# Transposing DMAs in place of TensorE for the normalised rows, with GpSimd taking half of the y rounding

## Chip, cores, metric

One core of a Trainium2 chip. The metric is the device time of one execution in microseconds (us), the median of several runs.

## What is computed

x is 4 x 2048 x 512 (batch, sequence, hidden), all in f32. Two branches start from the same normalised x and meet at the end:

```
xn  = layernorm(x)
q, k, v = xn @ Wq.T, xn @ Wk.T, xn @ Wv.T            # 512 -> 128 each
scan over the sequence:  r_t = q_t @ M.T ;  M = 0.99 * M + v_t.T @ k_t / b
s   = (r @ Wo.T) * sigmoid(gate)
h   = layernorm(xn) * gamma + beta
y   = silu(h @ dequant(fc1_q, fc1_scales) + fc1_bias)     # 512 -> 2048, scale groups of 128
z   = y @ dequant(fc2_q, fc2_scales) + fc2_bias           # 2048 -> 512, scale groups of 128
g   = silu(xn + 0.5 * z)
out = x + s * g
```

## The kernel before

The sequence is cut into 16 **chunks** of 128 steps: 4 batches x 128 steps are 512 rows, four tiles of 128. Precision is kept by splitting f32 operands into two f16 parts, a high one (the value rounded) and a low one (what rounding left), so most products are two or three f16 matmuls. Scales of groups are applied between partial sums: a bank is multiplied in place by a ratio before the next group is added to it.

Five instruction streams are written out by hand in **slots**, 64 to a chunk (`STEPS`), `G` counting all slots and `e` the slot in its chunk. No scheduler changes the order: what stands in a stream waits there, and all behind it waits too. The engines meet at semaphores only.

- **Every slot, TensorE**: one piece of fc1 (`ffn1`, L490, two matmuls) and one of fc2 (`ffn2`, L508, two matmuls). Block J of fc1 (128 of the 2048 features) takes four pieces two slots apart; even blocks have their last piece at slots 6, 14, 22, ..., odd blocks at 3, 11, 19, ... Two banks `blk` alternate between blocks.
- **ScalarE** multiplies each fc1 bank by its ratio (`rescale`, L636), which the next piece of that block waits for two slots later, and after the fourth piece makes y (`silu`, L643).
- **VectorE** multiplies each fc2 bank by its ratio (`block2_out`, L776; four banks, so TensorE wants each back after four slots), and splits y: `y_high` (L762) in the slot after silu, `y_low` (L767) in the slot after that. Both are needed by fc2 of the block, and `silu` of the block after next waits for `y_low`.
- **Side jobs, TensorE**: q at slot 3 (L439); for the four tiles, starting at slots 1, 13, 25, 37: kv (L450), kt (L455), scores (L460), read (L467 to L469) and wo (L475), 0, 4, 7, 10 and 13 slots after the start. They share two side banks.
- **Normalising the next chunk**: VectorE takes `stats` (L730) of x in slots 0 to 3 and `moments` (L733) in slots 5 and 6. GpSimd makes the row constants (`rows`, L1035 to L1045, then `row_scales`, L1053) and writes g = (x - mean) * scale into `g_rows` (`normalise`, L1060). TensorE **turns** g in slots 51, 54, 56, 59 (`turn`, L426): four transposes each into a side bank. From that bank ScalarE copies the high part (`g_high`, L583) and makes h (`h_whole`, L592), VectorE makes g's low part (`g_low`, L746), GpSimd splits h (`h_high` L1072, `h_low` L1076). fc1 of the next chunk needs h from its slot 0 on, kv and q need g from its slot 1 on.
- **Finishing the chunk before**, on GpSimd mostly: `prepare` (L1102, L1105) makes xn plus half the bias, `add_z` (L1110) adds z; ScalarE takes the last silu (`gate_silu`, L662, slots 16, 17, 21, 29); `output` (L1116, L1119) multiplies by s and adds x (slots 18, 22, 26, 30). GpSimd's order within a chunk is prepare 0 and 1, rows, add 0 and 1, prepare 2, add 2, prepare 3, output 0, add 3, outputs 1 to 3, four normalises, four splits of h.
- **SyncE** issues all loads and stores: of the next x (`load_x`, once g is made), of the x for the end (`load_again`), and the output.

In chunk 0 GpSimd, VectorE and ScalarE also unpack the fc2 weights; chunk 15 has no next chunk to normalise. The first chunk's g is turned before slot 0, in another place of the program (L547).

## Time and profile before

| | us |
|---|---|
| median of 3 runs | 1266.86 (1266.81 to 1268.67) |
| the profiled execution, its own time | 1264.73 |
| its span | 1262.8 |
| TensorE busy | 1190.5 (94%) |
| VectorE busy | 1143.2 (91%) |
| ScalarE busy | 914.7 (72%) |
| GpSimd busy | 784.3 (62%) |
| clock granted to TensorE | 0.993 of full |

The profiler's "busy" of TensorE counts the overlapping ends of pipelined matmuls, so the distance from one matmul's start to the next one's start says what it costs the stream. In the profile PE is TensorE, DVE VectorE, ACT ScalarE, POOL GpSimd, SP SyncE. `side`, `blk`, `blk2` are banks; the profile leaves buffer numbers out.

### The profile page before, as it was taken

How to read it: one execution, taken by the hardware profiler on the slowest of the kernel's cores; microseconds unless marked ns; L12 is line 12 of the kernel's file. 1: busy time of each engine (PE TensorE's matmuls, PEld its weight loads, DVE VectorE, ACT ScalarE, POOL GpSimd, SP SyncE). 2: the span in 40 equal slices, each digit the busy share in tenths (PEclk: the TensorE clock that was granted, in tenths of full speed). 3: DMA queues.
4: the chain of work that ended last, by engine and by line, in shares of the span. 5: the costliest groups of instructions: out<-in, count | busy, mean ns of one | idle time of the engine just before them, and what ended most of it. 6: DMA issues, size and time to landing. Idle time of an engine off the chain costs nothing.

```text
span 1262.8 us, 18949 instructions
## 1 busy us (share of the span) xinstructions
PE 1190.5 (94%) x6028; PEld 616.7 (49%) x6028; DVE 1143.2 (91%) x1969; ACT 914.7 (72%) x1590; POOL 784.3 (62%) x760
## 2 busy tenths in 40 slices
PE   2799999999999999999999999999999999999994
PEld 1344554555555555555555545555455545555551
DVE  8889989899998999999899998989999899999897
ACT  6788776777777767676777777677777776768672
...
DMA packets 41620, 65.68 MB, mean 52 GB/s; under 512 B 11696, under 2 KB 11952, under 8 KB 41008
## 3 DMA queue, kind: packets, MB, share of 16 engines
...
q10 hardware_dynamic: 288, 0.08, 0.0%
...
## 4 chain that ended last, share of the span: by engine, by line
PE 73%; DVE 12%; ACT 8%; issue 5%; POOL 1%; DMA 1%; SPq 0%; ACTq 0%; DVEq 0%
PE blk L490 27%; PE blk L508 25%; PE side L450 6%; DVE blk L776 5%; PE side L475 4%; PE side L439 3%; ACT blk L636 3%; PE side L467 2%; DVE y_split L767 2%; DVE tops L814 2%; ACT z_rows L662 1%; PE side L426 1%; DVE y_split L762 1%; PE side L468 1%; PE side L469 1%
## 5 line engine op out<-in xcount | busy, mean ns | idle before, releaser
L776 DVE TENSOR_TENSOR blk<-blk,ratio_rows 128x512 f32<-128x512 f32 x960 | 646.0, 692 | 79.4 <-PE blk L508 75.8
L636 ACT ACTIVATE blk<-blk,ratio 128x512 f32<-128x512 f32 x768 | 508.2, 666 | 228.9 <-PE blk L490 222.8
L490 PE MATMUL blk<-h_split,q_sb 128*128 128x512 f16 x2048 | 611.1, 380 | 12.1 <-ACT y_full L643 4.2
L508 PE MATMUL blk<-w_sb,y_split 128*128 128x512 f16 x2048 | 608.7, 379 | 2.5 <-POOL w_sb L1081 1.3
L508 PEld LDWEIGHTS blk<-w_sb,y_split 128*128 128x128 f16 x2048 | 199.4, 98 | 247.4 <-DVE blk L776 7.3
L490 PEld LDWEIGHTS blk<-h_split,q_sb 128*128 128x128 f16 x2048 | 194.4, 98 | 224.1 <-ACT blk L636 32.5
L643 ACT ACTIVATE y_full<-blk,par,last 128x512 f32<-128x512 f32 x256 | 201.6, 787 | 82.6 <-PE blk L490 81.9
L767 DVE SCALAR_TENSOR_TENSOR y_split<-y_full,up,y_split 128x512 f16<-128x512 f32 x256 | 220.6, 862 | 0.1
L1072 POOL CAST h_split<-h_full 128x512 f16<-128x512 f32 x64 | 52.6, 822 | 239.8 <-ACT h_full L592 239.8
L762 DVE TENSOR_SCALAR y_split<-y_full,up 128x512 f16<-128x512 f32 x256 | 170.1, 665 | 0.0
L1060 POOL TENSOR_SCALAR g_rows<-xt,mv,gs 128x512 f32<-128x512 f32 x60 | 133.1, 2227 | 0.0
L1116 POOL TENSOR_TENSOR z_rows<-z_rows,s_rows 128x512 f32<-128x512 f32 x62 | 92.2, 1488 | 58.7 <-ACT z_rows L662 58.7
L1110 POOL TENSOR_TENSOR z_rows<-z_rows,xz 128x512 f32<-128x512 f32 x60 | 90.3, 1513 | 12.0 <-DVE z_rows L781 10.8
L1119 POOL TENSOR_TENSOR z_rows<-z_rows,x_again 128x512 f32<-128x512 f32 x62 | 84.8, 1368 | 4.9
L1105 POOL TENSOR_TENSOR xz<-xz,b_half 128x512 f32<-128x512 f32 x60 | 83.2, 1386 | 5.0
L1076 POOL TENSOR_TENSOR h_split<-h_full,h_split 128x512 f16<-128x512 f32 x64 | 74.6, 1165 | 5.2
L450 PE MATMUL side<-wqkv_hi,g_hi 128*128 128x256 f16 x256 | 70.3, 275 | 1.5 <-DVE wqkv_lo L942 1.5
L450 PE MATMUL side<-wqkv_lo,g_hi 128*128 128x256 f16 x256 | 70.4, 275 | 0.0
L450 PE MATMUL side<-wqkv_hi,g_lo 128*128 128x256 f16 x256 | 70.4, 275 | 0.0
L781 DVE SCALAR_TENSOR_TENSOR z_rows<-blk,unit,ratio_rows 128x512 f32<-128x512 f32 x64 | 47.6, 744 | 22.3 <-PE blk L508 22.3
L475 PE MATMUL side<-wo_sb,s_mask 128*128 128x512 f32 x128 | 65.5, 593 | 0.5 <-DVE mem_t L756 0.5
L1102 POOL TENSOR_SCALAR xz<-x_again,row_z 128x512 f32<-128x512 f32 x60 | 56.9, 949 | 0.0
...
## 6 DMA issues: line engine op xcount, KB each, us to landing
xt<-in_x SPq DMA_DIRECT2D x64, 256.0 KB, 4.6
x_again<-in_x SPq DMA_DIRECT2D x256, 64.0 KB, 1.9
out<-z_rows SPq DMA_DIRECT2D x256, 64.0 KB, 1.7
...
```

The lines of the kernel that those rows point to most:

```text
L450: mm = pe.matmul(bank[:, 0:2 * M], a[:, k, rows], w[:, k, M:], start=(k == 0 and n == 0), stop=(k == KC - 1 and n == 2))
L475: pe.matmul(bank[:], r_t[:], wo_sb[:], start=True, stop=True).then_inc(wo_done, 1)
L490: mm = pe.matmul(blk[J % 2][:], q1_sb[:, g, j // 4, w, j % 4 * P:(j % 4 + 1) * P], a[:, c % 2, g, :], start=(g == 0 and n == 0), stop=(g = ...
L508: mm = pe.matmul(blk2[:, i, :], y[:, J % Y_RING, rows], w2_sb[:, j, part, :], start=(j == 0 and n == 0), stop=(j == FB - 1 and n == len(te ...
L636: act.activation(blk[J % 2][:], blk[J % 2][:], ACT.Copy, scale=ratio1[:, at:at + 1]).then_inc(blk_scaled, 1)
L643: act.activation(y_full[:, J % 2, :], blk[J % 2][:], ACT.Silu, bias=b1_c[:, j:j + 1], scale=last1[:, j:j + 1]).then_inc(silu_done, 1)
L762: dve.tensor_scalar(y_hi[:, J % Y_RING, :], y_full[:, J % 2, :], up_y, None, ALU.mult).then_inc(y_hi_done, 1)
L767: dve.scalar_tensor_tensor(y_lo[:, J % Y_RING, :], y_full[:, J % 2, :], up_y, y_hi[:, J % Y_RING, :], ALU.mult, ALU.subtract).then_inc(y_l ...
L776: dve.tensor_tensor(blk2[:, i, :], blk2[:, i, :], ratio2_rows[:, j, :], ALU.mult).then_inc(blk2_scaled, 1)
L1060: pool.tensor_scalar(g_rows[:, i, :], xt[:, i, :], mv[:, c % 2, i, 0:1], gs[:, c % 2, i:i + 1], ALU.subtract, ALU.mult).then_inc(g_done, 1)
L1110: pool.tensor_tensor(z_rows[:, i, :], z_rows[:, i, :], xz[:, i % 2, :], ALU.add).then_inc(z_sum, 1)
L1116: pool.tensor_tensor(z_rows[:, i, :], z_rows[:, i, :], s_rows[:, n % S_RING, :], ALU.mult).then_inc(z_mul, 1)
```

## The change

g no longer goes through TensorE, except for the first chunk. GpSimd's `normalise` writes g in place of x, in the form x * scale + shift, in slots 31, 33, 35, 37; the shift costs two more steps of `rows`, which moves from slot 7 to 9. ScalarE rounds the rows to the high part (`g_high`, slots 33 to 39), GpSimd subtracts (`g_low`, slots 34 to 40), and SyncE issues eight DMAs that transpose 128 x 512 of f16 each into `g_hi` and `g_lo` (`turn_g`). h is then made of g's two parts: `h_part` on ScalarE (slots 48, 50, 52, 54), `h_sum` on VectorE one slot later, the split on GpSimd one slot after that. `y_high` of odd blocks goes to GpSimd (`odd_y_high`), at slots 4, 12, 20, ..., and their `y_low` on VectorE from slot 5, 13, ... to slot 7, 15, ... The statistics stand at slots 0, 2, 4, 6, and the moments at 7 and 8.

```diff
-TURN_AT = (51, 54, 56, 59)
...
+G_HIGH_AT, G_LOW_AT = (33, 35, 37, 39), (34, 36, 38, 40)
+H_PART_AT, H_SUM_AT, H_SPLIT_AT = (48, 50, 52, 54), (49, 51, 53, 55), (50, 52, 54, 56)
...
-STATS_AT, MOMENTS_AT = (0, 1, 2, 3), (5, 6)
+STATS_AT, MOMENTS_AT = (0, 2, 4, 6), (7, 8)
...
-MASK_LAG, MEM_LAG, GLOW_LAG, YHIGH_LAG, YLOW_LAG = 1, 1, 3, 1, 2
-
-HSPLIT_LAG = 3
-NORMALISE_AT = (36, 38, 40, 42)
-PREPARE_AT, ROWS_AT, FIRST_ROWS_AT = (0, 3, 15, 18), 7, 28
+MASK_LAG, MEM_LAG, YHIGH_LAG, YLOW_LAG, ODD_YLOW_LAG = 1, 1, 1, 2, 4
+
+NORMALISE_AT = (31, 33, 35, 37)
+PREPARE_AT, ROWS_AT, FIRST_ROWS_AT = (0, 3, 15, 18), 9, 28
...
+        g_rows = xt
+        g_split = sb("g_split", [P, 2, NT, H], F16)
...
+            def turn_g(c):
+
+                sp.wait_ge(h_done, 4 * c)
+                sp.wait_ge(kv_done, 4 * c)
+                sp.wait_ge(q_done, c)
+                for i in range(NT):
+                    sp.wait_ge(g_lo_rows, NT * (c - 1) + i + 1)
+                    for n, to in enumerate((g_hi, g_lo)):
+                        sp.dma_start_transpose(to[:, :, i * P:(i + 1) * P], g_split[:, n, i, :]).then_inc(g_turned, 16)
...
                 if 0 < c < NCH - 1:
-                    g_wait(sp, c)
+                    sp.wait_ge(g_lo_rows, NT * c)
                     load_x(c + 1)
...
+                if c < NCH - 1:
+                    turn_g(c + 1)
...
+            def g_high(c, i):
+                act.wait_ge(g_done, NT * c + i + 1)
+
+                wait(act, g_turned, 2 * NT * 16 * (c - 1))
+                act.activation(g_split[:, 0, i, :], g_rows[:, i, :], ACT.Copy).then_inc(g_hi_rows, 1)
+
+            def h_part(c, k):
+                act.wait_ge(g_turned, 2 * NT * 16 * c)
+                act.wait_ge(h_done, 4 * c + k - 1)
+                act.activation(h_full[:, k % 2, :], g_hi[:, k, :], ACT.Identity,
+                               bias=beta_s[:, k:k + 1], scale=gamma_s[:, k:k + 1]).then_inc(h_part_done, 1)
...
+            def h_sum(c, k):
+                dve.wait_ge(h_part_done, 4 * (c - 1) + k + 1)
+                dve.scalar_tensor_tensor(h_full[:, k % 2, :], g_lo[:, k, :], gamma_s[:, k:k + 1], h_full[:, k % 2, :],
+                                         ALU.mult, ALU.add).then_inc(h_full_done, 1)
...
             def y_low(J):
-                dve.wait_ge(y_hi_done, J + 1)
+                if J % 2:
+                    dve.wait_ge(y_hi_odd_done, J // 2 + 1)
+                else:
+                    dve.wait_ge(y_hi_done, J // 2 + 1)
...
-                pool.tensor_tensor(nmr[:, c % 3, :], t[3], row_const[:, MINUS_ONE, :], ALU.mult
+                step(pool.tensor_tensor(nmr[:, c % 3, :], t[3], row_const[:, MINUS_ONE, :], ALU.mult))
+                step(pool.tensor_tensor(t[3], mean, gs[:, parity, :], ALU.mult))
+                pool.tensor_tensor(g_shift[:, parity, :], t[3], row_const[:, MINUS_ONE, :], ALU.mult
                                    ).then_inc(rows_done, 1)
...
-                    pool.wait_ge(turn_done, 4 * c)
-                pool.tensor_scalar(g_rows[:, i, :], xt[:, i, :], mv[:, c % 2, i, 0:1],
-                                   gs[:, c % 2, i:i + 1], ALU.subtract, ALU.mult).then_inc(g_done, 1)
+                pool.tensor_scalar(g_rows[:, i, :], xt[:, i, :], gs[:, c % 2, i:i + 1],
+                                   g_shift[:, c % 2, i:i + 1], ALU.mult, ALU.add).then_inc(g_done, 1)
+
+            def g_low(c, i):
+                pool.wait_ge(g_hi_rows, NT * (c - 1) + i + 1)
+                pool.tensor_tensor(g_split[:, 1, i, :], g_rows[:, i, :], g_split[:, 0, i, :], ALU.subtract
+                                   ).then_inc(g_lo_rows, 1)
...
+            def odd_y_high(J):
+                if J == 1:
+                    pool.wait_ge(y_scale, 1)
+                wait(pool, blk2_done, NT * (J - Y_RING + 1))
+                pool.wait_ge(silu_done, J + 1)
+                pool.tensor_scalar(y_hi[:, J % Y_RING, :], y_full[:, J % 2, :], up_y, 1.0, ALU.mult, ALU.mult
+                                   ).then_inc(y_hi_odd_done, 1)
```

Three places of the new order. On GpSimd, from the sum for the last tile of the chunk before (`add_z` of tile 3, slot 20) to the second normalise, before:

```order
L1110 TENSOR_TENSOR z_rows<-z_rows,xz 128x512 [waits z_out,xz_done]
L1116 TENSOR_TENSOR z_rows<-z_rows,s_rows 128x512 [waits s_out,z_silu]
L1119 TENSOR_TENSOR z_rows<-z_rows,x_again 128x512 [waits z_mul]
L1116 TENSOR_TENSOR z_rows<-z_rows,s_rows 128x512 [waits s_out,z_silu]
L1119 TENSOR_TENSOR z_rows<-z_rows,x_again 128x512 [waits z_mul]
L1116 TENSOR_TENSOR z_rows<-z_rows,s_rows 128x512 [waits s_out,z_silu]
L1119 TENSOR_TENSOR z_rows<-z_rows,x_again 128x512 [waits z_mul]
L1060 TENSOR_SCALAR g_rows<-xt,mv,gs 128x512 [waits turn_done,rows_done]
L1060 TENSOR_SCALAR g_rows<-xt,mv,gs 128x512 x3
```

and now (`y_split<-y_full` is the high half of an odd block):

```order
L1118 TENSOR_SCALAR y_split<-y_full,up 128x512 [waits silu_done,blk2_done]
L1149 TENSOR_TENSOR z_rows<-z_rows,xz 128x512 [waits z_out,xz_done]
L1155 TENSOR_TENSOR z_rows<-z_rows,s_rows 128x512 [waits s_out,z_silu]
L1158 TENSOR_TENSOR z_rows<-z_rows,x_again 128x512 [waits z_mul]
L1155 TENSOR_TENSOR z_rows<-z_rows,s_rows 128x512 [waits s_out,z_silu]
L1158 TENSOR_TENSOR z_rows<-z_rows,x_again 128x512 [waits z_mul]
L1118 TENSOR_SCALAR y_split<-y_full,up 128x512 [waits silu_done,blk2_done]
L1155 TENSOR_TENSOR z_rows<-z_rows,s_rows 128x512 [waits s_out,z_silu]
L1158 TENSOR_TENSOR z_rows<-z_rows,x_again 128x512 [waits z_mul]
L1084 TENSOR_SCALAR xt<-xt,gs,g_shift 128x512 [waits rows_done]
L1084 TENSOR_SCALAR xt<-xt,gs,g_shift 128x512
L1089 TENSOR_TENSOR g_split<-xt,g_split 128x512 [waits g_hi_rows]
```

Two high halves of y stand within this piece, a third ahead of it (slot 12), and g's low part follows the second normalise.

On ScalarE, slots 31 to 36 of the same chunk, now:

```order
L648 ACTIVATE blk<-blk,ratio 128x512 [waits blk_done] x3
L599 ACTIVATE g_split<-xt 128x512 [waits g_turned,g_done]
L648 ACTIVATE blk<-blk,ratio 128x512 [waits blk_done]
L655 ACTIVATE y_full<-blk,par,last 128x512 [waits y_lo_done,blk_done]
L599 ACTIVATE g_split<-xt 128x512 [waits g_turned,g_done]
L648 ACTIVATE blk<-blk,ratio 128x512 [waits blk_done]
```

The rescale of slot 34 stands behind a wait for the first normalise (`g_done`); before, no instruction of ScalarE stood behind `normalise` until slot 52.

On SyncE, now:

```order
L352 DMA x_again<-in_x 32x512 x4
L373 DMA_TRANSPOSE g_hi<-g_split 128x4x128 [waits q_done,g_lo_rows,kv_done,h_done]
L373 DMA_TRANSPOSE g_lo<-g_split 128x4x128
L373 DMA_TRANSPOSE g_hi<-g_split 128x4x128 [waits g_lo_rows]
L373 DMA_TRANSPOSE g_lo<-g_split 128x4x128
L373 DMA_TRANSPOSE g_hi<-g_split 128x4x128 [waits g_lo_rows]
L373 DMA_TRANSPOSE g_lo<-g_split 128x4x128
L373 DMA_TRANSPOSE g_hi<-g_split 128x4x128 [waits g_lo_rows]
L373 DMA_TRANSPOSE g_lo<-g_split 128x4x128
L345 DMA xt<-in_x 32x4x512 [waits g_lo_rows]
```

The load of the next x, which stood behind the normalises alone, now stands behind the eight transposing DMAs, and these behind kv of the last tile (slot 37).

## Rows read from the trace of the kernel before

**Rows 1.** Page, span and busy time of each engine.

```profile
span 1262.8 us, 18949 instructions
PE 1190.5 (94%) x6028; PEld 616.7 (49%) x6028; DVE 1143.2 (91%) x1969; ACT 914.7 (72%) x1590; POOL 784.3 (62%) x760
```

**Rows 2.** Stretches of one chunk each: length, busy time by engine, clock, DMA.

```profile
485.34:560.22 74.88, 73.58 (x377) 38.40 (x377) 68.39 (x117) 55.05 (x98) 48.90 (x47) 1.00 0.16 43
560.22:635.10 74.88, 73.58 (x376) 38.37 (x377) 68.39 (x117) 55.06 (x98) 48.90 (x47) 1.00 0.17 43
```

**Rows 3.** Chain of waits, 605 to 640 us: start, us, what.

```profile
606.06 0.43 PE blk L490 x2
606.50 0.43 PE blk L508 x2
...
626.71 0.44 PE side L426 x4
...
632.20 0.39 DVE y_split L762
632.59 0.61 DVE blk L776
633.19 0.65 DVE y_split L767
...
634.45 0.60 DVE g_lo L746
...
635.10 0.66 PE side L426 x4
```

**Rows 4.** TensorE by time, fc1 of slots 0, 8, 36, fc2 of slot 6.

```profile
564.49 0.60 PE L490 MATMUL blk<-h_split,q_sb 128*128 128x512 f16 x2 [0.16 <-ACT y_full L643]
...
574.12 0.59 PE L508 MATMUL blk<-w_sb,y_split 128*128 128x512 f16 x2
...
575.42 0.59 PE L490 MATMUL blk<-h_split,q_sb 128*128 128x512 f16 x2
...
608.71 0.59 PE L490 MATMUL blk<-h_split,q_sb 128*128 128x512 f16 x2
```

**Rows 5.** GpSimd by time, 576 to 615 us: start, us, line, [idle before it].

```profile
576.23 0.20 POOL L1035 TENSOR_TENSOR v<-mv,row_const 128x4 f32<-128x4 f32 x1 [5.34 <-DVE mv L733]
...
581.82 0.20 POOL L1045 TENSOR_TENSOR row_z<-v,row_const 128x4 f32<-128x4 f32 x1
...
585.53 0.77 POOL L1102 TENSOR_SCALAR xz<-x_again,row_z 128x512 f32<-128x512 f32 x1
586.39 1.27 POOL L1105 TENSOR_TENSOR xz<-xz,b_half 128x512 f32<-128x512 f32 x1
...
591.58 1.27 POOL L1116 TENSOR_TENSOR z_rows<-z_rows,s_rows 128x512 f32<-128x512 f32 x1
592.92 1.33 POOL L1119 TENSOR_TENSOR z_rows<-z_rows,x_again 128x512 f32<-128x512 f32 x1
...
603.27 1.66 POOL L1116 TENSOR_TENSOR z_rows<-z_rows,s_rows 128x512 f32<-128x512 f32 x1 [1.68 <-ACT z_rows L662]
...
606.51 8.86 POOL L1060 TENSOR_SCALAR g_rows<-xt,mv,gs 128x512 f32<-128x512 f32 x4
```

**Rows 6.** VectorE by time, the last moments of the chunk.

```profile
575.92 0.24 DVE L733 BATCH_NORM_AGGREGATE mv<-stat 128x2 f32<-128x6 f32 x2
```

**Rows 7.** Groups by line and shape: busy us, mean ns of one, idle before.

```profile
L583 ACT ACTIVATE g_hi<-side 128x512 f16<-128x512 f32 x60 | 36.1, 602 | 0.0
L1145 POOL TENSOR_SCALAR b_half<-b_half 128x512 f32<-128x512 f32 x1 | 1.5, 1512 | 0.0
```

**Rows 8.** y's low half on VectorE: shortest, median and longest in ns.

```profile
L767 DVE SCALAR_TENSOR_TENSOR y_split<-y_full,up,y_split x256: 735/747/1648, 47.4 to 1241.6; 128x512 f16<-128x512 f32 x128
```

**Rows 9.** DMA issues: KB each, us to landing; then SyncE by time.

```profile
xt<-in_x SPq DMA_DIRECT2D x64, 256.0 KB, 4.6
x_again<-in_x SPq DMA_DIRECT2D x256, 64.0 KB, 1.9
...
596.07 1.83 SPq L349 DMA_DIRECT2D x_again<-in_x  x4
```

More of the change, by code:

```diff
@@ L20 @@
 TOP = 2.0 ** 14
-ROW_STEPS = 10
+ROW_STEPS = 12
 TINY = 1e-30
@@ L69 @@
         SIDE[TILE_AT[_i] + JOB_AT[_n]] = (_job, _i)
-    SIDE[TURN_AT[_i]] = ("turn", _i)
 def build(nc, x, wqkv, wo, gate, m0, q1, q2, b2, params, out):
@@ L91, in side_job @@
             return None
-        job, i = SIDE[e]
-        c += 1 if job == "turn" else 0
-        return (job, c, i) if c < NCH and not (job == "turn" and c == 0) else None
+        return (SIDE[e][0], c, SIDE[e][1]) if c < NCH else None
     def job_behind(G, lag, kind):
@@ L106, in finishing, with next_chunk @@
         return (c - 1, at.index(e)) if c > 0 and e in at else None
+    def next_chunk(G, at):
+        c, e = divmod(G, STEPS)
+        return (c + 1, at.index(e)) if c < NCH - 1 and e in at else None
     def fc1_step(G):
@@ L417, in bank_free @@
                     pe.wait_ge(s_out, n)
-                else:
-                    pe.wait_ge(g_lo_done, n)
-            def turn(c, k, bank):
-                if k == 0:
-                    g_wait(pe, c)
-                for i in range(NT):
-                    mm = pe.transpose(bank[:, i * P:(i + 1) * P], g_rows[:, i, k * P:(k + 1) * P], ident[:])
-                mm.then_inc(turn_done, 1)
             def run_side(G):
@@ L432, in run_side @@
                 bank_free(G)
-                if job == "turn":
-                    turn(c, i, bank)
-                elif job == "q":
+                if job == "q":
                     for k in range(KC):
@@ L442, in run_side @@
                 elif job == "kv":
-                    if i == 0:
-                        pe.wait_ge(g_lo_done, 4 * c + 4)
+                    if i == 0 and c == 0:
+                        pe.wait_ge(g_lo_done, 4)
+                    elif i == 0:
+                        pe.wait_ge(g_turned, 2 * NT * 16 * c)
                     if c == 0 and i == 0:
@@ L682, in _ @@
             for k in range(KC):
-                h_whole(0, k, first_turn_bank[k])
-                g_high(0, k, first_turn_bank[k])
+                first_h(k, first_turn_bank[k])
+                first_g_high(k, first_turn_bank[k])
             act.wait_ge(wqkv_scale, 1)
@@ L717, in _ @@
                     s_copy(*at, side[JOB_BANK[G - S_LAG]])
-                if at := job_behind(G, GHIGH_LAG, "turn"):
-                    g_high(*at, side[JOB_BANK[G - GHIGH_LAG]])
-                if at := job_behind(G, HFULL_LAG, "turn"):
-                    h_whole(*at, side[JOB_BANK[G - HFULL_LAG]])
+                if at := next_chunk(G, G_HIGH_AT):
+                    g_high(*at)
+                if at := next_chunk(G, H_PART_AT):
+                    h_part(*at)
                 if at := finishing(G, GATE_AT, LAST_GATE_AT):
@@ L924, in _ @@
             top_of_q1(3).then_inc(tops_made, 1)
-            g_low(0, 0, first_turn_bank[0])
+            first_g_low(0, first_turn_bank[0])
             pick(OF_Q1)
-            g_low(0, 1, first_turn_bank[1])
+            first_g_low(1, first_turn_bank[1])
             largest(OF_Q1, top_q1[:])
@@ L975, in _ @@
                     mask_scores(*at, side[JOB_BANK[G - MASK_LAG]])
-                if at := job_behind(G, GLOW_LAG, "turn"):
-                    g_low(*at, side[JOB_BANK[G - GLOW_LAG]])
+                if at := next_chunk(G, H_SUM_AT):
+                    h_sum(*at)
                 if at := job_behind(G, MEM_LAG, "read"):
                     remember(*at, side[JOB_BANK[G - MEM_LAG]])
-                if (at := fc1_step(G - YHIGH_LAG) if G >= YHIGH_LAG else None) and at[1] == KC - 1:
+                if (at := fc1_step(G - YHIGH_LAG) if G >= YHIGH_LAG else None) and at[1] == KC - 1 and at[0] % 2 == 0:
                     y_high(at[0])
-                if (at := fc1_step(G - YLOW_LAG) if G >= YLOW_LAG else None) and at[1] == KC - 1:
+                if (at := fc1_step(G - YLOW_LAG) if G >= YLOW_LAG else None) and at[1] == KC - 1 and at[0] % 2 == 0:
+                    y_low(at[0])
+                if (at := fc1_step(G - ODD_YLOW_LAG) if G >= ODD_YLOW_LAG else None) and at[1] == KC - 1 and at[0] % 2:
                     y_low(at[0])
@@ L1148, in _ @@
                 c, e = divmod(G, STEPS)
+                if (at := fc1_step(G - YHIGH_LAG) if G >= YHIGH_LAG else None) and at[1] == KC - 1 and at[0] % 2:
+                    odd_y_high(at[0])
                 if G - Q2_LOW_LAG in Q2_AT:
@@ L1161, in _ @@
                     row_scales(c + 1)
-                if c < NCH - 1 and e in NORMALISE_AT:
-                    normalise(c + 1, NORMALISE_AT.index(e))
-                if at := job_behind(G, HSPLIT_LAG, "turn"):
+                if at := next_chunk(G, NORMALISE_AT):
+                    normalise(*at)
+                if at := next_chunk(G, G_LOW_AT):
+                    g_low(*at)
+                if at := next_chunk(G, H_SPLIT_AT):
                     h_high(*at)
```

47 lines of the change are left out of this document (21 added, 26 removed).

## The prediction

> **What bounds the kernel now.** I read the page's busy times first: TensorE is busy for 94% of the span, VectorE for 91%, GpSimd for 62% [rows 1]. Stretches of one chunk each then show a steady state: two chunks in a row last 74.88 us, at full clock, with the same counts [rows 2]. So the sum can be made for one chunk. The chain of waits shows what such a chunk is: in most slots TensorE follows TensorE, 0.43 us for the two matmuls of fc1 and 0.43 us for those of fc2 [rows 3]. Where the turns stand the chain leaves TensorE: a turn costs the stream 0.44 us when its bank is free, and before the fourth it waits for `g_low`, 0.66 instead of 0.44 us in the chain, with about 0.34 us lost at that place [rows 3]. Slot 0 loses about 0.33 us more behind a silu (TensorE idle, released by ScalarE) [rows 4]. The last view is GpSimd by time. It waits 5.34 us for the moments, starts the row constants at 576.23 us, and from there to the first normalise at 606.51 us is idle once, for 1.68 us before the last product [rows 5]. That stretch is the one to keep in mind: nobody waits for its end now, since g is turned only at 626.71 us [rows 3]. A measurement of this kernel can tell changes of about 0.2% (2.5 us) from none.
>
> **What TensorE gains.** Four turns of 0.44 us leave each chunk: 1.76 us. With them goes the 0.34 us before the fourth. The 0.33 us at slot 0 comes from ScalarE being crowded by eight extra instructions between slots 52 and 61; it has the same eight afterwards, four (`g_high`) in slots 33 to 39 and four (`h_part`) in slots 48 to 54, so I take it to go and put 0.3 us back for new small waits. Gain if nothing else gets in the way: 1.76 + 0.34 + 0.33 - 0.30 = 2.1 us a chunk.
>
> **What VectorE gains, priced at nothing.** It loses eight `y_high` of 0.39 us and four `g_low` of 0.60 us a chunk and gets four `h_sum`; by its operands the nearest row to that is `y_low`, 0.65 us [rows 3]. That is about 3 us less in 68.4 us of work [rows 2]. It is hidden by TensorE except around the turns, counted above. If the gain did not come, the cover is the four slots for which a bank of fc2 may be away.
>
> **What moves onto the path: GpSimd between slots 8 and 33.** `g_high` on ScalarE stands in slot 33 and waits for the first normalise. The rescale of slot 34 stands behind it, and TensorE needs that rescale for fc1 in slot 36. So a late normalise stops TensorE. I count from the start of slot 8 (575.42 us now [rows 4]).
>
> - The moments end two slots later than now. VectorE starts from the fc2 product of slot 6 (574.12 + 0.63 us [rows 4]) and has three scalings of 0.61, one statistics of about the same, one `y_high` 0.39, two `y_low` 0.65 and two pairs of moments of 0.24 [rows 3, 6]: done near 579.4 us, 3.9 us after the start of slot 8. Now it is 576.2 us.
> - GpSimd's stretch now takes 606.51 - 576.23 = 30.3 us; without the idle 1.68 it is 28.6 us of work [rows 5]. Added are two row steps of 0.28 us each (a 0.20 us step and the gap to the next), three high halves of y (slots 12, 20, 28), and the first normalise itself, which must now be complete. The new normalise has the form of L1102, multiply and add with two columns of scalars: 0.77 us [rows 5], a third of the old one's 8.86 / 4. For the high half no row has two multiplies. The nearest from below is L1102, 0.77 us; the old normalise (subtract, multiply) took 2.2 us, and the one single multiply, L1145, 1.51 us [rows 5, 7]. I take 0.77, the row with the same count of operations and a multiply first, and keep 2.2 for a rival. Sum: 28.6 + 0.56 + 2.31 + 0.77 = 32.2 us.
> - Part of the 28.6 is mutual hindrance. `y_low` takes 735 ns at the shortest and up to 1648 ns [rows 8], and GpSimd's own instructions are stretched next to VectorE's. Unhindered, the stretch has 6.1 us of row constants, two preparations of 0.77 + 1.27 and their gaps (2.1), four outputs of 1.27 + 1.33 (2.6) and four adds of 1.3 [rows 5], together 25.9 instead of 28.6: then 29.5 instead of 32.2. Fewer `y_high` on VectorE take a part of the 2.7 us away, I say a quarter: 31.5 us.
> - Behind it: `g_high` 0.60 us [rows 7], one rescale of about 0.6, a semaphore's delay: 1.3 us.
>
> Slot 36 then starts 3.9 + 31.5 + 1.3 = 36.7 us after slot 8. Now it is 608.71 - 575.42 = 33.3 us [rows 4]. That is 3.4 us lost a chunk; smaller waits on the way (the gate's silu in slots 16 and 17 behind `add_z`, `y_low` of slot 23 behind the high half of slot 20) fall inside it, because GpSimd is late, not held up by them.
>
> The Trainium skill says in "SBUF — State Buffer", on contention, that VectorE and GpSimd share one port pair as an exclusive lock, held for a whole instruction, when VectorE runs a two-port mode or reads two SBUF tensors. By that rule `h_sum` (two SBUF inputs) brings new collisions with the splits of h in slots 49 to 56, and an odd `y_high` on VectorE was one itself; the spread of `y_low` agrees with it. It changes the 0.3 us put back above, perhaps to 1.
>
> **The transposing DMAs.** Eight of 128 KB each chunk. They may start when kv of the last tile is done, about 3.2 us after slot 36 starts, and must all have landed when ScalarE comes to `h_part` in slot 48, about 14.7 us after it: a window of 11.5 us. The last pair is released by the fourth `g_low` some 7 us before its end. No transposing DMA is in the trace. From below: an issue costs SyncE 1.83 / 4 = 0.46 us and 64 KB land in 1.9 us, 256 KB in 4.6 us [rows 9]; one after the other issued, overlapping in flight, the eight fit. From above: eight that each take 4.6 us alone need 36.8 us. I take them to fit, since the DMA engines are only 16 to 17% busy [rows 2], and price them at nothing; the cover is the 11.5 us. The next load of x, queued behind them, lands in 4.6 us and is wanted a good 15 slots later.
>
> **Sum.** A steady chunk: 3.4 - 2.1 = +1.3 us, 74.9 to 76.2. There are 14 such chunks: +18. Chunk 0 has nothing to finish and keeps 2.1 us of gain; chunk 15 has no normalise but the odd high halves among its GpSimd work, about +1.5. Together +17: the profiled execution's 1264.7 becomes 1282, and the median, which lies 2.1 us above it, 1284.
>
> **Rivals.**
> - **GpSimd is in time (faster).** Place: slot 33. The first normalise decides; ScalarE gets there about 29.4 us after slot 8 and has 1 us to spare, so at 30.4 us nothing is lost and at 35.4 (my 3.9 + 31.5) the 3.4 us are. Unhindered it is 33.4, slot 36 is 1.4 us later instead of 3.4, and the sum is -0.7 a chunk: 14 of them and the -0.6 of the two ends give 1256. If the stretch is shorter still, because the moments come as early as now or the hindrance was mine to overrate, up to 2.1 us a chunk come in, 15 x 2.1 = 32: 1235. For it: TensorE is the busiest engine and its work shrinks for certain. Against: the stretch is already without gaps and only gets longer.
> - **The high half of y is slow on GpSimd.** At 1.5 to 2.2 us instead of 0.77 the three in the stretch add 2.2 to 4.3 us a chunk: 1284 + 14 x 2.2 = 1315 to 1344. For it: two of the three nearest rows. Against: the fast one shares its opening multiply by a column of scalars.
> - **The transposes are late.** They decide once the eight take over 11.5 us. At 1.9 us each, one after the other, they take 15.2: 3.7 us more a chunk, 15 times: 1340. At 4.6 us each it is 25 us a chunk, beyond 1600. For it: no row shows one overlapping another. Against: the idle DMA engines.
>
> The Trainium skill's page "VectorE: DVE Perf Modes", in "The three transpose paths", gives 1309 ns for a 128 x 128 square of 2-byte values by DMA against 390 ns on TensorE, and prefers TensorE; should that be a cost in sequence, the 32 squares of a chunk would need an estimated 42 us, near the worst of this rival. The page "DMA: Bandwidth & Descriptors" gives 261 GB/s for one kernel's DMA transposes, by which a chunk's megabyte would take an estimated 4 us, which fits.
>
> **How the numbers follow.** Forecast 0.45, its own range 1260 to 1304 (a stretch near 29.8, and 32.2 with 1 us of new waits). In time: 0.27, 1235 to 1260. Slow high half: 0.12. Late transposes: 0.16, half of that beyond 1345. The range 1238 to 1342 leaves out less than 2 in 10. Faster by over 0.2%: 0.27 and a sixth of the forecast, 0.34. Within 0.2%: 0.08, from the forecast. Slower: 0.58.
>
> **What would show it.** Right: ScalarE idle before `g_split<-xt` of slot 33, released by GpSimd, some 3 us, and TensorE's wait for the rescale behind it; GpSimd without a gap from the row constants to the normalise; a steady chunk of 76 us. Wrong: a chunk under 74 us with that idle time absent; `y_split<-y_full` on GpSimd over 1.2 us; ScalarE idle before `h_full<-g_hi`, released by a DMA, which would be the transposes.

## The result, and the profile after

The change takes **1353.4 us** (median of four runs, 1352.4 to 1354.2) against 1266.9 for the kernel before: 1.0681 times as long, interval 1.0668 to 1.0694. Forecast were 1284 and a range of 1238 to 1342. The sign is right; the loss is 87 us where 17 were forecast.

The page of the changed kernel, its span, busy times and the chain by engine (before: [rows 1]):

```profile
span 1351.8 us, 18739 instructions
PE 1192.6 (88%) x5788; PEld 590.6 (44%) x5788; DVE 1124.2 (83%) x1842; ACT 927.9 (69%) x1590; POOL 861.4 (64%) x980
...
PE 42%; POOL 23%; DVE 18%; issue 12%; ACT 4%; DMA 1%; POOLq 0%; SPq 0%; ACTq 0%; DVEq 0%
```

TensorE is no longer at 94% but at 88%, and no other engine has taken its place as the busiest. Less than half of the chain is TensorE's. That is the picture of engines that wait for one another. Two chunks, each from the start of its slot 0 to the start of the next slot 0 (length, busy time by engine, clock, DMA; before: [rows 2]):

```profile
527.09:606.79 79.70, 72.41 (x362) 36.23 (x361) 67.12 (x109) 55.82 (x98) 53.47 (x61) 1.00 0.23 54
606.79:687.95 81.16, 74.10 (x362) 36.71 (x361) 66.90 (x109) 56.00 (x98) 53.66 (x61) 0.98 0.22 53
```

There are two kinds of chunk now. Of chunks 1 to 14, five take 79.7 us with the clock at 1.00, and nine 81.0 to 81.2 us with the clock at 0.98; before, all took 74.9 at 1.00. Together the fourteen take 1128.8 us instead of 1048.4, 80 of the 89 us that the span is longer; chunk 0 takes 90.5 instead of 83.3. So most of the loss lies in the steady chunk: 4.8 us in each, and 1.5 us more where the clock fell. The view of waits (engine, line, for whom; us in all, times, longest):

```profile
POOL v L1058 <- DVE mv L745: 125.9, 15, 8.8
POOL h_split L1101 <- DVE h_full L761: 108.4, 29, 7.0
...
DVE y_split L786 <- POOL y_split L1118: 44.4, 14, 3.2
PEld side L480 <- DVE mem_t L772: 43.3, 15, 3.0
...
PE side L480 <- DVE mem_t L772: 35.9, 15, 2.5
...
ACT h_full L604 <- POOL h_split L1105: 19.9, 15, 1.5
...
ACT g_split L599 <- POOL xt L1084: 15.1, 15, 1.3
```

Once in each chunk VectorE waits 3.2 us in `y_low` (L786) for GpSimd's high half (L1118), and once TensorE waits 2.5 to 3 us in wo (L480) for VectorE's memory update (L772). The wait that the prediction named, ScalarE before `g_split<-xt` (L599), is there too, at 1.0 us rather than 3. The timelines of one chunk (the second above) show how the first two hang together. GpSimd:

```profile
621.62 0.20 POOL L1058 TENSOR_TENSOR v<-mv,row_const 128x4 f32<-128x4 f32 x1 [8.42 <-DVE mv L745]
...
637.74 1.44 POOL L1155 TENSOR_TENSOR z_rows<-z_rows,s_rows 128x512 f32<-128x512 f32 x1
639.26 1.27 POOL L1158 TENSOR_TENSOR z_rows<-z_rows,x_again 128x512 f32<-128x512 f32 x1
640.51 0.69 POOL L1118 TENSOR_SCALAR y_split<-y_full,up 128x512 f16<-128x512 f32 x1
...
650.12 1.27 POOL L1155 TENSOR_TENSOR z_rows<-z_rows,s_rows 128x512 f32<-128x512 f32 x1 [1.10 <-ACT z_rows L674]
...
652.73 2.70 POOL L1084 TENSOR_SCALAR xt<-xt,gs,g_shift 128x512 f32<-128x512 f32 x2
```

VectorE in the same place:

```profile
637.50 0.56 DVE L778 TENSOR_SCALAR y_split<-y_full,up 128x512 f16<-128x512 f32 x1
641.24 1.74 DVE L786 SCALAR_TENSOR_TENSOR y_split<-y_full,up,y_split 128x512 f16<-128x512 f32 x1 [3.17 <-POOL y_split L1118]
642.90 0.69 DVE L795 TENSOR_TENSOR blk<-blk,ratio_rows 128x512 f32<-128x512 f32 x1
643.50 0.27 DVE L772 SCALAR_TENSOR_TENSOR mem_t<-mem_t,side 128x128 f32<-128x128 f32 x1
```

And TensorE:

```profile
643.83 1.60 PE L480 MATMUL side<-wo_sb,s_mask 128*128 128x512 f32 x2 [2.54 <-DVE mem_t L772]
645.22 1.06 PE L495 MATMUL blk<-h_split,q_sb 128*128 128x512 f16 x2
```

The high half of slot 20 stands on GpSimd behind two steps of an output tile and starts at 640.51. VectorE has come to the low half (slot 23) at 638.07 and stands for 3.17 us. Behind it in VectorE's queue, after one scaling of a bank, is the 0.27 us memory update. It reads the bank into which wo of slot 26 will write, so TensorE waits for it. A product of GpSimd that is late by three microseconds stops TensorE through two queues.

What follows the wait differs. In the chunk before, the same wait of 2.54 us stands before the same wo, and the matmuls behind it run at full speed:

```profile
564.13 1.12 PE L480 MATMUL side<-wo_sb,s_mask 128*128 128x512 f32 x2 [2.54 <-DVE mem_t L772]
565.09 0.59 PE L495 MATMUL blk<-h_split,q_sb 128*128 128x512 f16 x2
```

In the chunk of the timelines the clock that TensorE was granted stood at half (1.2 of 2.4 GHz) for 3.4 us from then on; the stretch:

```profile
644.23:647.64 3.41, 3.41 (x8) 1.06 (x7) 2.09 (x4) 1.32 (x2) 3.33 (x3) 0.52 0.37 99
```

The pair of fc1 takes 1.06 us there instead of 0.59, and the three slots 26 to 28 lose 4.5 us instead of 2.8. This happened in nine of the fourteen chunks. What decides whether the clock falls after this wait, these runs do not show.

To add up such places in every kernel I use one measure: the length of a slot between the starts of its fc1 matmuls, less 0.86 us for fc1 and fc2 and the shortest time its side job takes. What is left is TensorE's loss in that slot. Summed over a chunk, worked out from TensorE's timeline, for chunks 2 to 14, in us. Where a kernel has chunks with the clock under 1.00, they stand behind a stroke, with how many of chunks 1 to 14 they are:

| kernel | median us | chunk | lost in slots 8 to 40 | lost in 41 to 63 | turns |
|---|---|---|---|---|---|
| before | 1266.9 | 74.9 | 2.0 | 0.7 | 1.8 |
| the change | 1353.4 | 79.7 / 81.2 (9) | 6.1 (2.8 in 26 to 28) / 7.6 (4.1 to 4.5) | 3.2 | 0 |
| e1, y on VectorE | 1316.6 | 76.7 / 78.1 to 78.4 (11) | 4.3 (2.5 in 35 to 37) / 5.7 to 6.0 (3.9 to 4.2) | 2.0 | 0 |
| e2, statistics early | 1308.7 | 77.0 to 77.6 | 3.4 to 4.0 | 3.2 | 0 |
| e3, DMAs alone | 1269.4 | 74.8 to 75.4 | 2.4 | 2.0 to 2.6 | 0 |
| e4, low half later | 1366.4 | 80.0 / 81.4 to 81.8 (12) | 5.7 (2.6 in 35 to 37) / 7.1 to 7.4 (4.0 to 4.3) | 4.0 | 0 |
| e5, before + odd y | 1294.7 | 76.8 | 3.4 | 1.2 | 1.8 |
| e6, before + late statistics | 1291.2 | 76.6 | 3.7 | 0.7 | 1.8 |
| e7, before + new normalise | 1269.3 | 75.0 | 2.0 | 0.7 | 1.8 |
| e8, later h | 1269.3 | 74.8 | 3.4 (1.6 in 11) | 1.0 | 0 |
| e10, mask first | 1247.6 | 72.8 to 73.9 | 1.1 | 1.3 to 2.4 | 0 |
| e11, before + mask first | 1275.9 | 75.4 | 1.8 (1.0 in 27) | 1.4 | 1.8 |
| e12, change + mask first | 1353.8 | 79.6 to 79.8 / 80.2 to 82.2 (10) | 6.6 (3.1 in 27 to 29) / 7.1 to 8.5 | 2.6 to 3.3 | 0 |

Each chunk less its three losses gives 70.3 to 70.5 us, so little is left out.

### The profile page after: what moved, and what is told of

Its sections match the earlier page's. It is cut to its first block, busy times and chain, and to the rows that moved or that the text cites. A ratio compares the mean times of both kernels' runs of the same rounds, so it can differ in the third digit from the quotient of the medians.

```text
span 1351.8 us, 18739 instructions
## 1 busy us (share of the span) xinstructions
PE 1192.6 (88%) x5788; PEld 590.6 (44%) x5788; DVE 1124.2 (83%) x1842; ACT 927.9 (69%) x1590; POOL 861.4 (64%) x980
## 4 chain that ended last, share of the span: by engine, by line
PE 42%; POOL 23%; DVE 18%; issue 12%; ACT 4%; DMA 1%; POOLq 0%; SPq 0%; ACTq 0%; DVEq 0%
PE blk L495 16%; PE blk L513 15%; DVE blk L795 7%; DVE y_split L786 5%; PE side L455 3%; POOL z_rows L1149 3%; PE side L442 3%; POOL xz L1144 3%; POOL y_split L1118 3%; PE side L480 3%; POOL h_split L1105 2%; POOL xz L1141 2%; DVE y_split L778 2%; POOL z_rows L1155 1%; POOL h_split L1101 1%
## 5 line engine op out<-in xcount | busy, mean ns | idle before, releaser
L795 DVE TENSOR_TENSOR blk<-blk,ratio_rows 128x512 f32<-128x512 f32 x960 | 630.6, 688 | 103.1 <-PE blk L513 101.0
L495 PE MATMUL blk<-h_split,q_sb 128*128 128x512 f16 x2048 | 621.3, 386 | 43.2 <-ACT blk L648 37.3
L648 ACT ACTIVATE blk<-blk,ratio 128x512 f32<-128x512 f32 x768 | 502.6, 661 | 223.9 <-PE blk L495 213.2
L786 DVE SCALAR_TENSOR_TENSOR y_split<-y_full,up,y_split 128x512 f16<-128x512 f32 x256 | 246.0, 961 | 44.5 <-POOL y_split L1118 44.4
L1118 POOL TENSOR_SCALAR y_split<-y_full,up 128x512 f16<-128x512 f32 x128 | 99.4, 776 | 132.0 <-ACT y_full L655 102.3
L1101 POOL CAST h_split<-h_full 128x512 f16<-128x512 f32 x64 | 43.0, 673 | 108.4 <-DVE h_full L761 108.4
L480 PE MATMUL side<-wo_sb,s_mask 128*128 128x512 f32 x128 | 69.5, 626 | 35.9 <-DVE mem_t L772 35.9
L1089 POOL TENSOR_TENSOR g_split<-xt,g_split 128x512 f16<-128x512 f32 x60 | 72.2, 1203 | 39.3 <-ACT g_split L599 39.3
L1105 POOL TENSOR_TENSOR h_split<-h_full,h_split 128x512 f16<-128x512 f32 x64 | 86.0, 1343 | 5.3
L778 DVE TENSOR_SCALAR y_split<-y_full,up 128x512 f16<-128x512 f32 x128 | 83.1, 649 | 0.6 <-ACT y_full L655 0.6
L1149 POOL TENSOR_TENSOR z_rows<-z_rows,xz 128x512 f32<-128x512 f32 x60 | 78.6, 1320 | 2.9 <-DVE z_rows L800 1.7
L761 DVE SCALAR_TENSOR_TENSOR h_full<-g_lo,gamma_s,h_full 128x512 f32<-128x512 f16 x60 | 62.7, 1045 | 11.2 <-ACT h_full L604 11.2
L455 PE MATMUL side<-wqkv_hi,g_hi 128*128 128x256 f16 x256 | 70.3, 275 | 1.5 <-DVE wqkv_lo L961 1.5
```

Of the source, the lines that this page charges most:

```text
L455: mm = pe.matmul(bank[:, 0:2 * M], a[:, k, rows], w[:, k, M:], start=(k == 0 and n == 0), stop=(k == KC - 1 and n == 2))
L495: mm = pe.matmul(blk[J % 2][:], q1_sb[:, g, j // 4, w, j % 4 * P:(j % 4 + 1) * P], a[:, c % 2, g, :], start=(g == 0 and n == 0), stop=(g = ...
L648: act.activation(blk[J % 2][:], blk[J % 2][:], ACT.Copy, scale=ratio1[:, at:at + 1]).then_inc(blk_scaled, 1)
L778: dve.tensor_scalar(y_hi[:, J % Y_RING, :], y_full[:, J % 2, :], up_y, None, ALU.mult).then_inc(y_hi_done, 1)
L786: dve.scalar_tensor_tensor(y_lo[:, J % Y_RING, :], y_full[:, J % 2, :], up_y, y_hi[:, J % Y_RING, :], ALU.mult, ALU.subtract).then_inc(y_l ...
L795: dve.tensor_tensor(blk2[:, i, :], blk2[:, i, :], ratio2_rows[:, j, :], ALU.mult).then_inc(blk2_scaled, 1)
```

## The experiments

**The three parts apart (e1, e2, e3).** e1 is the change with all high halves of y back on VectorE; `y_low` takes its old lag of two slots.

```
-                if J % 2:
-                    dve.wait_ge(y_hi_odd_done, J // 2 + 1)
-                else:
-                    dve.wait_ge(y_hi_done, J // 2 + 1)
+                dve.wait_ge(y_hi_done, J + 1)
...
-                if (at := fc1_step(G - YHIGH_LAG) if G >= YHIGH_LAG else None) and at[1] == KC - 1 and at[0] % 2 == 0:
+                if (at := fc1_step(G - YHIGH_LAG) if G >= YHIGH_LAG else None) and at[1] == KC - 1:
...
-                if (at := fc1_step(G - YHIGH_LAG) if G >= YHIGH_LAG else None) and at[1] == KC - 1 and at[0] % 2:
-                    odd_y_high(at[0])
```

> The change, with all high halves of y back on VectorE (and the low half of odd blocks back in the slot it had). Theory 1, VectorE stands behind GpSimd: in the profile of the change y_low of slot 23 waits 3.2 us for GpSimd's high half of slot 20, and wo in slot 26 waits for the memory update behind it; that is 3 to 4 us of the 10.6 us that TensorE loses in a chunk, and the splits of h in slots 50 to 61 share GpSimd with two more high halves. Without them: the losses at slots 26 to 28 gone, those at 54 to 61 down from 2.8 to about 1, a later first normalise left: a chunk of 75 to 76 us, the run at 1265 to 1285. Theory 2, the transposing DMAs are what costs: no or little help, over 1335.

e2 is the change with the statistics back in their places, and e3 has both edits:

```
-STATS_AT, MOMENTS_AT = (0, 2, 4, 6), (7, 8)
-PREPARE_AT, ROWS_AT, FIRST_ROWS_AT = (0, 3, 15, 18), 9, 28
+STATS_AT, MOMENTS_AT = (0, 1, 2, 3), (5, 6)
+PREPARE_AT, ROWS_AT, FIRST_ROWS_AT = (0, 3, 15, 18), 7, 28
```

> The change, with statistics in slots 0 to 3, moments in 5 and 6 and the row constants at slot 7 as before. Theory 1: GpSimd's stretch begins about 2 us earlier, so the waits behind it shrink by about 2 us a chunk, and the loss at slot 11 (1.1 us, the mask behind the moments) goes back to 0.3: 81.2 to 78 us a chunk, the run at 1300 to 1315. Theory 2 (DMAs): unchanged, 1350.

> The change with both undone: only g's path through GpSimd, ScalarE and the transposing DMAs is left. Theory 1: TensorE's losses fall to 3 to 4 us a chunk, 73.5 to 75 us, the run at 1245 to 1270; the eight DMAs (1.27 us of issue each on SyncE and 2.5 us to land, 13 us from the last kv) now end later than slot 48 wants them, and ScalarE waits about 1 us there. Theory 2: above 1330, with a long wait of ScalarE for the DMAs.

Measured, as ratios to the kernel before: e1 (1316.6 us, a miss: 1265 to 1285 were expected) 1.0394 (1.0364 to 1.0423), e2 1.0318 (1.0301 to 1.0335), e3 1.0021 (1.0010 to 1.0032). The DMA path alone is within 2.2 us of the kernel before. The late statistics add 47 us to it (1316.6 against 1269.4), the odd high halves 39 (1308.7), and the change is 84 above e3, about the sum of the two. So **the loss is that of the two riders, not of the transposing DMAs.** Part of it came by the clock: in e1 eleven chunks with the clock at 0.98 last 1.4 to 1.7 us longer than those at 1.00, about 18 of its 47 us, and in the change nine by 1.5 us make 13 of its 87. e2 and e3 have no steady chunk with a fallen clock.

The waits of e1 show the mechanism of the prediction by itself. Without odd high halves there is no wait between VectorE and GpSimd over y, and ScalarE waits 3.0 us a chunk for the normalise:

```profile
ACT g_split L599 <- POOL xt L1079: 45.0, 15, 3.2
...
ACT h_full L604 <- POOL h_split L1100: 5.9, 12, 0.8
```

e2 shows what the odd high halves do in the second half of the chunk:

```profile
ACT h_full L604 <- POOL h_split L1105: 20.1, 15, 1.4
...
PEld side L480 <- DVE mem_t L772: 8.3, 10, 1.0
```

ScalarE's `h_part` waits for a split of h on GpSimd 1.3 us in each chunk, as in the change (19.9 us in 15), and 5.9 in all without the high halves. TensorE loses 1.2 us more in slots 41 to 63 (3.2 against 2.0). In the changed kernel the place is this, ScalarE first; behind `h_part` stands the rescale (L648) that TensorE needs:

```profile
679.89 0.81 ACT L604 ACTIVATE h_full<-g_hi,beta_s,gamma_s 128x512 f32<-128x512 f16 x1 [1.37 <-POOL h_split L1105]
```

```profile
681.31 0.60 PE L495 MATMUL blk<-h_split,q_sb 128*128 128x512 f16 x2 [1.52 <-ACT blk L648]
```

The wait of wo for the memory update, 2.9 us a chunk in the change, is 8.3 us over the whole run here, and e1 has no such wait among its long ones: at its full length it needs both riders, a GpSimd that is late and a high half in its queue.

**The wait taken out of the change (e4).** The low half of an odd block comes one slot later and behind the memory update, so the update is no longer queued behind it.

```
-MASK_LAG, MEM_LAG, YHIGH_LAG, YLOW_LAG, ODD_YLOW_LAG = 1, 1, 1, 2, 4
+MASK_LAG, MEM_LAG, YHIGH_LAG, YLOW_LAG, ODD_YLOW_LAG = 1, 1, 1, 2, 5
```

> The change, with y_low of odd blocks one slot later on VectorE, behind the memory update of slot 24 instead of ahead of it. Theory 1: wo of slot 26 no longer waits; what is left is silu of slot 27, which waits for the same y_low, so 1 to 2 us a chunk come back: 1322 to 1340. If the loss at slot 26 had another cause, it stays and the run is at 1350 or slower.

Missed: 1366.4 us, ratio 1.0774 (1.0756 to 1.0792), slower than the change, in chunks at full clock (80.0 against 79.7) as in the others. The waits tell why:

```profile
ACT g_split L599 <- POOL xt L1084: 47.2, 15, 3.4
DVE y_split L786 <- POOL y_split L1118: 31.2, 14, 2.2
...
ACT y_full L655 <- DVE y_split L786: 24.6, 32, 1.2
```

The memory update hardly appears any more as a releaser of wo (0.8 us, once in the run). But ScalarE now waits 3.1 us a chunk for the normalise instead of 1.0, and TensorE's loss has moved from slots 26 to 28 to slots 35 to 37. A later low half also holds the next silu (24.6 us). So GpSimd's lateness is paid in the main once a chunk, at whichever consumer comes first. Taking one consumer away gave nothing back. The clock fell here in twelve chunks, behind the wait in slot 35, where it fell in nine of the change.

**The riders on the kernel before (e5, e6) and the new normalise (e7).** e5 puts only the odd high halves on GpSimd, with the code of the change; e6 sets only `STATS_AT`, `MOMENTS_AT` and `ROWS_AT` as the change does; e7 gives the old kernel the multiply-add normalise with its two extra row steps:

```
-                pool.tensor_scalar(g_rows[:, i, :], xt[:, i, :], mv[:, c % 2, i, 0:1],
-                                   gs[:, c % 2, i:i + 1], ALU.subtract, ALU.mult).then_inc(g_done, 1)
+                pool.tensor_scalar(g_rows[:, i, :], xt[:, i, :], gs[:, c % 2, i:i + 1],
+                                   g_shift[:, c % 2, i:i + 1], ALU.mult, ALU.add).then_inc(g_done, 1)
```

> The kernel before, with only the odd high halves of y on GpSimd and their low halves two slots later. Theory 1 (VectorE and TensorE stand behind GpSimd's unbroken stretch, whose length counts): the stretch from the row constants starts as early as before, and the high halves of slots 12, 20 and 28 lengthen it by 2.1 us; y_low of slot 23 waits, and wo of slot 26 or slot 27 behind it, 1 to 2 us a chunk; VectorE's relief around the turns gives some 0.5 back. 1275 to 1295. Rival (VectorE was the bound and is relieved): 1250 to 1262.

> The kernel before, with only the statistics spread to slots 0 to 6, the moments at 7 and 8 and the row constants at 9. Theory 1: GpSimd's stretch begins 2 to 3 us later, but behind it stand only the gate's silu of slots 16, 17 and 21, not y; TensorE loses the 0.8 us at slot 11 and up to 1 us at slots 17 to 23 in each of 15 chunks: 1275 to 1290. If the late start alone were worth what it was in the change (45 us there), 1305 or more.

> The kernel before, with only the new form of the normalise (multiply and add, with the two extra row steps). GpSimd gets 4 x 1.4 us back a chunk after its stretch and loses 0.56 us in it. Nobody waits for the end of the old normalises before slot 51, so both theories say no change: 1264 to 1270. It would be faster only if the long normalises hinder VectorE around slots 33 to 41.

Measured: e5 1.0219 (1.0204 to 1.0235), 28 us; e6 1.0191 (1.0176 to 1.0207), 25 us, just above its range; e7 1.0019 (1.0009 to 1.0028). Each rider costs about 2% even where g is turned on TensorE and nobody needs a normalise in slot 33. With the DMA path, which needs it there, late statistics cost 47 instead of 25, but some 18 of the 47 are the clock's, which did not fall in a steady chunk of e5 or e6. e7 gains nothing, though GpSimd has shorter normalises: TensorE's losses only move (slot 23 from 0.95 to 0.15 us, slot 35 from 0.43 to 1.30).

**The transposes priced (e9).** e3 with the steps on h four slots earlier, so that the first `h_part` stands in slot 44. There is one run of it.

```
-H_PART_AT, H_SUM_AT, H_SPLIT_AT = (48, 50, 52, 54), (49, 51, 53, 55), (50, 52, 54, 56)
+H_PART_AT, H_SUM_AT, H_SPLIT_AT = (44, 46, 48, 50), (45, 47, 49, 51), (46, 48, 50, 52)
```

> The version with only g's path by DMA, with h four slots earlier (h_part in slots 44 to 50). It prices the transposes: eight issues of 1.31 us and 2.5 us of landing are 13 us from the last kv, and slot 44 comes 7 to 8 us after it. If the eight issues are serial, ScalarE waits 5 to 6 us a chunk for the DMAs: 1340 to 1360. If they overlapped more than the profile says, under 1290.

1335.0 us in that run, a little under the expected 1340 to 1360; the wait:

```profile
ACT h_full L604 <- DMA g_lo<-g_split: 63.3, 15, 4.9
```

Now the transposes are late, by 4.2 us a chunk, with the sign that the prediction had named: ScalarE idle before `h_full<-g_hi`, released by a DMA. (The clock stood at 0.96 to 0.98 in all fourteen of its steady chunks, so its time is not the price of the DMAs alone.) In the changed kernel that wait is 1.0 us in all, in two chunks. SyncE's timeline of the changed kernel gives the price:

```profile
659.86 1.22 SPq L373 DMA_TRANSPOSE g_hi<-g_split  x1
661.12 1.26 SPq L373 DMA_TRANSPOSE g_lo<-g_split  x1
...
667.67 1.27 SPq L373 DMA_TRANSPOSE g_hi<-g_split  x1
668.98 1.27 SPq L373 DMA_TRANSPOSE g_lo<-g_split  x1
```

```profile
g_hi<-g_split SPq DMA_TRANSPOSE x60, 2.5
g_lo<-g_split SPq DMA_TRANSPOSE x60, 2.5
```

One issue holds SyncE for 1.27 us, 1.31 from start to start; the last of eight starts 9.1 us after the first and lands 2.5 us later (second fence, the page's DMA issues). That is 11.6 us against the 11.5 us window of the prediction: just in time, by luck rather than by the argument given.

**What bounds the DMA path alone (e8, e10, e11, e12).** e8 is e3 with the steps on g and h later, to see whether the losses in slots 41 to 63 go:

```
-G_HIGH_AT, G_LOW_AT = (33, 35, 37, 39), (34, 36, 38, 40)
-H_PART_AT, H_SUM_AT, H_SPLIT_AT = (48, 50, 52, 54), (49, 51, 53, 55), (50, 52, 54, 56)
+G_HIGH_AT, G_LOW_AT = (35, 37, 39, 41), (36, 38, 40, 42)
+H_PART_AT, H_SUM_AT, H_SPLIT_AT = (49, 52, 55, 58), (50, 53, 56, 59), (51, 54, 57, 60)
```

> The version with only g's path by DMA, with ScalarE's high parts of g two slots later (35 to 41) and the three steps of h three slots apart (49 to 60). Theory 1: its losses at slot 35 (1.3 us, ScalarE waiting for the first normalise) and at slots 54 to 61 (1.6 us, h_sum on VectorE beside GpSimd's split) shrink by about half each: 74.8 to 73.4 us a chunk, 1240 to 1255, below both kernels. Rival: GpSimd's lateness only moves to the next wait, 1265 to 1270.

Missed: 1.0023 (1.0014 to 1.0033), the same as e3. The late loss fell from 2.0 to 1.0 us, and the loss in slot 11 rose from 0.6 to 1.6. Slots 11 and 35 are `read` (L472), which needs the mask, and the mask stands in VectorE's queue behind the outputs of fc2. e10 is e8 with VectorE's mask ahead of them and the read one slot later:

```
-TILE_AT, JOB_AT = (1, 13, 25, 37), (0, 4, 7, 10, 13)
+TILE_AT, JOB_AT = (1, 13, 25, 37), (0, 4, 7, 11, 14)
...
+                if at := job_behind(G, MASK_LAG, "scores"):
+                    mask_scores(*at, side[JOB_BANK[G - MASK_LAG]])
                 if at := fc2_step(G):
                     block2_out(*at)
-                if at := job_behind(G, MASK_LAG, "scores"):
-                    mask_scores(*at, side[JOB_BANK[G - MASK_LAG]])
```

> The version with g by DMA and the later h, with VectorE's mask of the scores ahead of the bank scaling of its slot instead of behind it, and the read (and wo) on TensorE one slot later. Theory 3, formed from the last runs: what TensorE still loses, 1.6 us at slot 11 and 1.3 us at slot 35, is the read waiting for a mask that stands in VectorE's queue behind instructions stretched by GpSimd. Then about 2 to 2.5 us a chunk come back: 74.8 to 72.6 us, 1230 to 1245, below both kernels. Rival: VectorE as a whole is behind, and the loss moves to the banks of fc2: 1262 to 1270.

e10 takes 1247.6 us, ratio 0.9849 (0.9835 to 0.9864): **faster than both kernels**, by 1.5% than the one before, though not the expected 1230 to 1245. The weight loads of the read show where the time came from, e3 first and then e10:

```profile
PEld side L472 <- issue: 41.3, 48, 1.5
```

```profile
PEld side L472 <- issue: 10.8, 29, 0.8
```

Which of its two edits did more was not tried apart. In e10 the transposes are late, 20.1 us in 14 chunks before `h_part` (L604), and TensorE loses 0.4 to 1.5 us of each chunk behind it in slot 51. The same edits on e7 (with the first turn in slot 52) and on the change:

> The same two edits (mask first, read and wo a slot later; the first turn at slot 52) on the kernel before with the new form of the normalise. Its losses at slots 11, 23 and 35 are 1.66 us a chunk in all; by theory 3 1 to 1.6 us of them come back: 1243 to 1254, so that the DMA path keeps an advantage of about 10 us over it (1.76 us a chunk of turns, less its own waits). Rival: 1262 to 1268.

> The same two edits on the change itself. Its loss of 4 us at slots 26 to 28 comes from the memory update behind y_low behind GpSimd, not from the mask; wo moves from slot 26 to 27 and meets the same wait 0.9 us later. Theory 1 and 3: the losses at 11 and 35 (2.5 us) come back in part, those at 26 to 28 fall by under 1 us: 1315 to 1340. If GpSimd's stretch alone set the chunk, no gain: 1350.

Both missed: e11 takes 1275.9 us, 1.0067 (1.0053 to 1.0080), and e12 1353.8, 1.0684 (1.0665 to 1.0704), no gain at all. In e12 the wait for the memory update is still there, one slot later, 2.9 us a chunk, and the odd high halves still hold VectorE:

```profile
DVE y_split L786 <- POOL y_split L1118: 55.0, 28, 3.2
PEld side L480 <- DVE mem_t L772: 48.9, 17, 3.3
```

In e11 slot 27 (wo of the second tile) loses 1.0 us; its cause was not followed. So the order of e10 pays with the DMA path and without the riders; the gain is not that of the missing turns alone (e3 and e8 have none either), and why the order pays only there stays open.

## Why the prediction was wrong

In the measure of the table, the forecast was +3.4 us in slots 8 to 40, +0.3 - 0.34 - 0.33 in the rest, and -1.76 of turns: +1.3. Measured in a chunk at full clock are +4.1, +2.4 and -1.8: +4.8, and in nine chunks 1.5 more. Over chunks 1 to 14 that is 80 us where 18 were forecast. Of the 62 that are missing, 39 are the second section's (14 x 2.8), 13 the clock's (9 x 1.5) and 10 the first section's (14 x 0.7). Chunk 0 lost 7 us where 2.1 of gain were forecast; only a part of it is the clock (0.94 there, 0.98 before), the rest was not followed.

- **The turns of 1.76 us: right.** They are gone, and nothing replaces them on TensorE.
- **"Put 0.3 us back for new small waits": the step that failed.** This term had no row behind it, and it is 3.2 us in the change. 2.0 are there in e3, without a rider, and 1.0 in e8, where the steps of h stand three slots apart instead of two: so in e3 the DMA path's own gain of 2.1 us a chunk came down to 0.1 (74.8 against 74.9). A further 1.2 come with the odd high halves (e2), through GpSimd's splits of h, for which ScalarE waits. For `h_sum` the prediction took the 0.65 us by which `y_low` holds VectorE in the chain (0.75 by the median duration [rows 8]); it lasts 1.05 on the mean. The high half of y stands at 1.13 us between two splits:

```profile
L761 DVE SCALAR_TENSOR_TENSOR h_full<-g_lo,gamma_s,h_full 128x512 f32<-128x512 f16 x60 | 62.7, 1045 | 11.2 <-ACT h_full L604 11.2
```

```profile
674.52 0.61 POOL L1101 CAST h_split<-h_full 128x512 f16<-128x512 f32 x1 [7.00 <-DVE h_full L761]
675.22 1.16 POOL L1105 TENSOR_TENSOR h_split<-h_full,h_split 128x512 f16<-128x512 f32 x1
676.36 1.13 POOL L1118 TENSOR_SCALAR y_split<-y_full,up 128x512 f16<-128x512 f32 x1
677.44 0.60 POOL L1101 CAST h_split<-h_full 128x512 f16<-128x512 f32 x1
678.13 1.67 POOL L1105 TENSOR_TENSOR h_split<-h_full,h_split 128x512 f16<-128x512 f32 x1
```

- The same cast takes 0.60 us, but the product of h 1.16 or 1.67, and `y_low` 0.74 to 1.77 us over the run, 961 ns on the mean against 862 before. The Trainium skill, "SBUF — State Buffer", on contention, has VectorE and GpSimd lock a shared port pair, by which the prediction gave this term "perhaps 1". The durations agree with hindrance between the two, but no run takes it away by itself, so its share of the 3.2 us stays open.
- **The clock was taken as full throughout: the second step that failed.** Rows 2 showed 1.00, and no term asks what a new wait does to it. It fell to half in nine chunks, each time behind the wait of wo.
- **"The smaller waits on the way ... fall inside it, because GpSimd is late, not held up by them": right in the sum at full clock, wrong where the clock fell.** In the chunk that starts at 527.09 us GpSimd has no gap, the first normalise is done 35.2 us after the start of slot 8 (forecast 35.4), and slot 36 starts after 37.4 (forecast 36.7). So the 2.8 us of slot 26 lie inside the 3.4 us and not beside them; e4 shows the same, for there they turn up in slot 35. But the first consumer of the late GpSimd is not ScalarE in slot 33, which waits 1.0 us instead of 3. It is VectorE in slot 23, with the memory update behind it, and wo behind that. There TensorE waits 2.54 us in one piece. Where the clock fell upon it, ScalarE's silu of the gate came late in its turn, GpSimd did wait for it (1.10 us), and the normalise was done after 36.4 us.
- **VectorE "priced at nothing": wrong by the 0.7 us of the first section.** The last wait before slot 36 is not for the rescale. It is the read of slot 35, for a mask that VectorE, by then busy without a gap, makes late. The profile names no releaser there, but the code lets the read wait for the mask, which is done at 574.59 us. VectorE first:

```profile
574.31 0.28 DVE L767 TENSOR_TENSOR s_mask<-side,mask 128x128 f32<-128x128 f32 x1
```

```profile
574.69 0.46 PE L472 MATMUL side<-q_t,mem_t 128*128 128x128 f32 x2 [1.33 <-issue]
```

- **The moments in slots 7 and 8 were priced for GpSimd only.** Slot 11, the read, loses 1.1 us instead of 0.3, and 1.5 in e1 and e6. The likely reason is that VectorE's statistics and moments now stand nearer to the mask that the read needs: e2 has them early, and loses 0.5. No sentence of the prediction counts it; counted from slot 8 it lies inside the 3.4 us.
- **The time of GpSimd's stretch: right.** Moments done 3.8 us after slot 8 (forecast 3.9); from the row constants to the end of the first of the two normalises 31.3 us at full clock (31.5), 32.5 where the clock fell.
- **GpSimd in time: refuted.** ScalarE waits for the first normalise in all 15 chunks that have one.
- **The slow high half: refuted.** It was the cheap end of the bounds:

```profile
L1118 POOL TENSOR_SCALAR y_split<-y_full,up x128: 682/690/1128, 52.5 to 1328.0; 128x512 f16<-128x512 f32 x128
```

- **The late transposes: refuted as the cause** by e3, which has the same DMAs and is 2.2 us above the kernel before, and true in e9, where the window is shorter. The Trainium skill's page "VectorE: DVE Perf Modes" gives 1309 ns for one square of 128 by 128. Here one DMA of four squares is issued every 1.31 us, so the estimated 42 us of a cost in sequence were four times too much. Its preference for TensorE cannot be judged by one kernel: e10 turns g by DMA and is faster than the kernel before, but for that one no order was tried beside those of e5 to e7 and e11.
